# Second attention: ACT copies the bank turned one step earlier, then makes the exponential

## What is computed

```python
scores = (einsum('bhsc,btc->bhst', q_abs, kv) + einsum('bhsd,bxtd->bhst', q_pe, k_pe)) * SCALE
scores = where(causal, scores, finfo.min)
attn = softmax(scores, axis=-1)
x = einsum('bhst,btc->bhsc', attn, kv)
```

## Time and profile before

| | us |
|---|---|
| median of 3 runs | 1374.88 (1374.29 to 1378.86) |
| the profiled execution | 1376.57 |
| its span in the profile | 1374.8 |
| TensorE busy, share of the span | 1207.0, 88% |
| DVE busy | 887.0, 65% |
| ACT busy | 729.8, 53% |
| POOL busy | 535.7, 39% |
| mean granted TensorE clock | 0.932 |

### The profile page before, as it was taken

The page is one execution under the profiler, slowest core; times in us unless marked ns, Lnnn a source line. Parts: engine busy times, 40 slices in busy tenths (PEclk is TensorE's granted clock), DMA queues, the critical chain, the costliest instruction groups (busy, mean ns, idle before and its releaser), DMA issues. The chain is left out here.

```text
span 1374.8 us, 22122 instructions
## 1 busy us (share of the span) xinstructions
PE 1207.0 (88%) x7424; PEld 858.3 (62%) x7424; DVE 887.0 (65%) x2307; ACT 729.8 (53%) x1681; POOL 535.7 (39%) x561
## 2 busy tenths in 40 slices
PE   4798739999999889878599999999999999999878
PEld 3586714444444477667467777677767777676667
DVE  7767548899998345535477666667677666667501
ACT  2376303687777425453366656666666656665400
POOL 1244233435441100523065555455565555455200
PEclk9798855899999997999799999999999999999989
DMA  6670175446440285010211111101011111100091
GB/s 186 124 140 15 54 103 67 52 60 101 58 57 25 68 225 150 12 40 16 84 28 42 43 43 43 43 16 55 20 39 43 43 43 43 43 17 16 32 327 40
DMA packets 111057, 91.43 MB, mean 67 GB/s; under 512 B 49568, under 2 KB 101088, under 8 KB 109152
## 3 DMA queue, kind: packets, MB, share of 16 engines
q1 hardware_dynamic: 110944, 90.01, 28.6%
HBM read 50.92 MB, written 30.67 MB: 59 GB/s over the span
## 5 line engine op out<-in xcount | busy, mean ns | idle before, releaser
L988 POOL TENSOR_SCALAR a_p<-a_p,a_rl 128x128 f32<-128x128 f32 (+7 forms) x256 | 216.8, 849 | 332.0 <-DVE a_rl L930 331.7
L971 ACT ACTIVATE a_p<-psum,a_nm 128x128 f32<-128x128 f32 (+7 forms) x256 | 189.7, 741 | 58.4 <-DVE a_nm L924 56.7
L1485 ACT ACTIVATE a_pt<-psum 128x512 f32<-128x512 f32 (+3 forms) x384 | 168.1, 493 | 76.5 <-PE psum L1345 73.5
L1027 PE MATMUL psum<-ident,a_p 128*128 128x128 f32 x1152 | 175.7, 280 | 13.9 <-DVE a_pt L957 13.9
L957 DVE COPY a_pt<-psum 128x512 f32<-128x512 f32 (+1 forms) x192 | 114.6, 597 | 101.2 <-PE psum L1027 100.6
L955 ACT ACTIVATE a_pt<-psum 128x256 f32<-128x256 f32 (+2 forms) x192 | 87.6, 456 | 156.6 <-PE psum L1027 156.6
L1027 PEld LDWEIGHTS psum<-ident,a_p 128*128 128x128 f32 x1152 | 127.2, 140 | 62.6 <-issue 48.1
L1054 PE MATMUL psum<-a_pt,v 128*64 128x256 f32 (+1 forms) x1280 | 159.4, 370 | 2.3 <-ACT a_ot L1068 2.3
L1335 PE MATMUL psum<-a_op_k,a_op_q 64*128 64x512 f32 (+3 forms) x384 | 137.1, 456 | 23.8 <-DVE a_op_k L1451 22.7
L1345 PE MATMUL psum<-a_op_q,a_op_k 64*128 64x512 f32 (+3 forms) x384 | 129.9, 421 | 8.0 <-ACT a_pt L1485 6.1
L1345 PEld LDWEIGHTS psum<-a_op_q,a_op_k 64*128 64x128 f32 x384 | 64.1, 197 | 103.5 <-ACT a_pt L1485 86.8
(11 more groups left out here) (338 smaller groups left out, 2772.3 us busy)
## 6 DMA issues: line engine op xcount, KB each, us to landing
a_swap<-w_p SPq DMA_DIRECT2D x64, 128.0 KB, 2.3
ot_d<-a_ot SPq DMA_DIRECT2D x16, 512.0 KB, 4.5
o_ot<-ot_d SPq DMA_DIRECT2D x8, 1024.0 KB, 9.6
a_raw_q<-qk_d SPq DMA_DIRECT2D x48, 128.0 KB, 4.7
room<-qk_d SPq DMA_DIRECT2D x48, 128.0 KB, 7.8
w<-wf_d SPq DMA_DIRECT2D x16, 384.0 KB, 3.3
qk_d<-d_stage_h SPq DMA_DIRECT2D x64, 64.0 KB, 2.1
qk_d<-d_stage_l SPq DMA_DIRECT2D x64, 64.0 KB, 2.1
```

The source lines that it names most:

```text
L971: e.activation(s.p[:, t % NPB, 0:(i + 1) * P], C.score[t % 2][:, 0:(i + 1) * P], ACT.Exp, scale=-1.0, bias=s.nm[:, k:k + 1], accum_out=s.l ...
L988: e.tensor_scalar(s.p[:, t % NPB, 0:(i + 1) * P], s.p[:, t % NPB, 0:(i + 1) * P], s.rl[:, k:k + 1], 1.0, ALU.mult, ALU.mult).then_inc(s.no ...
L1027: ins = e.transpose(C.turn[par][:, (k - k0) * P:(k - k0 + 1) * P], s.p[:, tt % NPB, k * P:(k + 1) * P], C.ident[:, :])
L1485: e.activation(pt[:, k // G0 % NPT, hd, off:HALF], bank_b("score", g, k)[:, off:HALF], ACT.Exp, scale=-1.0).then_inc(exped, 1)
```

## The change

ACT's copy of a turned bank in slot t is that of the unit turned in slot t-1, not in slot t. DVE has had this order in all slots but the last of a group. The exponential of step t stays where it is, behind the copy of its slot; the output copy stays ahead of both. At the end of the stage the slots that run on after the last step (10 of them) take the copies that are left. Nothing is added or removed: as many copies, of the same shapes, with the same semaphores and counts, each a slot later in ACT's program.

```diff
 def softmax_act(e, C, s, n, t, later):
     core = s.core
     S = n * core.SI + t
-    evacuate(e, C, s, n, t, later, 1)
+    evacuate(e, C, s, n, t - 1, later, 1)
     if t < core.SI:
         c, hd, i = core.steps[t % core.SG]
         k = t % NST
```

## The result

The changed kernel takes 1405.51 us in the median of its runs (1399.15 to 1408.6), against 1375.38 for the kernel before in the runs beside it: a ratio of 1.0207, 95% interval 1.0176 to 1.0237. It is slower by 2.1%, 30.1 us between the medians. Its profiled execution took 1406.48 us, with a span of 1404.7, 29.9 more than the 1374.8 of before.

A forecast was written before the change was run, and what follows sets the result against it. TensorE was taken to bound the stage. 16 groups x 0.96 us (slot 12), 15 boundaries x 0.96 (slot 0) and 0.33 for the tail gave 30.1: median 1405.0 us, own range 1400 to 1409, wider range 1389 to 1416.

The forecast's parts named there:

- The mechanism: Slots 12 and 0: TensorE's odd-bank transposes wait for ACT's later copy (line 955), delaying the scores; 31 waits in all.
- both places: Slot 12, before score(13), and slot 0, before score(1): each 0.96 us late; slot 12 alone costing had chance 0.04, slot 0 alone 0.13.
- turn(15): TensorE's turn in slot 15: expected still to wait about 0.84 us for DVE, not absorbing slot 12's delay.
- The gain: Exponentials no longer waiting for their own slot's turn: value 0, bounds 0 and 13 us; rival "faster" had chance 0.05.
- The price of a place: Slots 12 and 0: delay of the next score by the later copy, its lag and the odd transposes, 0.96 us each.
- the lag from the end of ACT's copy to the transpose: Slots 12 and 0: taken as 0.15 us, from the tail's value products that waited for an ACT copy.
- The two checks beside it: Times from the ends of exp(11) and exp(15) to the scores waiting for them: 0.14 and 0.15 us.
- The edges: First group, last stretch and tail: late places at 0.96 us each, and 0.33 us for the tail.
- the tail: After the last group: value products 0.59 us later, last products 0.26 us earlier, +0.33 us in all.
- 1.00 throughout: TensorE's granted clock, expected to be still 1.00 in the changed kernel's trace.
- The sum: Whole stage: 15.4 us for slot 12, 14.4 for slot 0 and 0.33 for the tail, 30.1 us; chance 0.70.
- The walk past the other places: Other odd banks: turn(14) closest, 0.08 us late but hidden, copy(12) with more in hand; value 0, third-place rival 8 us, 0.08.

The follow-up runs named there:

- e3: Changed kernel's order, but the odd banks of slots 11 and 15 copied in their own slots again; 1375.46 us, ratio 1.0007 against the kernel before.
- e4: Kernel before, with only the odd banks of slots 11 and 15 copied a slot late; 1399.73 us, ratio 1.0199.
- e7: Kernel before, with ACT copying the even banks of slots 14 and 15, and odd banks of slots 5, 7, 9 a slot late; 1351.79 us.
- e1: Changed kernel's order, but slot 11's odd bank copied in its own slot again; 1385.24 us, ratio 1.0087 against the kernel before.
- e8: Kernel before, with ACT copying the even banks of slots 14 and 15, and slot 12's odd bank a slot late; 1356.67 us.
- e5: Changed kernel, with the output copy behind the bank copy in every slot; 1392.35 us, ratio 1.0144 against the kernel before.

## Why the prediction was right, and where its numbers were not

**The mechanism** held at both places. TensorE waits for line 955 in slots 12 and 0, at no other place of a regular group; exp(11) and exp(15) start when DVE is done, no earlier against their scores than before; turn(15) still waits 0.84 for DVE, so the delay of slot 12 passes through DVE's chain whole. e3 and e4 show both halves by themselves.

**The gain** was taken as 0 and is 0.07 us in each regular group, 1 us in all, and 0.75 in the last group. Between score(8) and score(9) 1.39 us lie in the trace of before (850.89 and 852.28) and 1.34 in the changed one (779.26 and 780.60); e7 gets 0.06 back from slots 5, 7 and 9 alone. I had called exp(11) and exp(15) the only exponentials that count, since I took every row of waiting to be theirs. exp(7) ended at the moment at which TensorE wanted it and held it up by less than a row shows.

In the last group it was a misreading of the earlier trace rows. Of the 15 waits of the matmul row for an exponential, one of 0.40 us is ahead of score(5) of the last group, for exp(3), which stands behind the copy of its own slot's bank. With that copy late (e3) the wait is gone, and score(5) starts 0.65 us earlier after turn(15) of the 15th group: 10.93 instead of 11.58. Rows of the kernel before, then of e3:

```profile
1264.77 0.60 ACT L955 ACTIVATE a_pt<-psum 128x512 f32<-128x512 f32 x1 [1.34 <-PE psum L1027]
1265.26 0.47 ACT L971 ACTIVATE a_p<-psum,a_nm 128x256 f32<-128x256 f32 x1
...
1265.88 0.50 PE L1006 MATMUL psum<-k10h,a_q10h 128*128 128x512 f32 x1 [0.40 <-ACT a_p L971]
```

```profile
1260.83 0.60 ACT L955 ACTIVATE a_pt<-psum 128x512 f32<-128x512 f32 x1 [0.46 <-PE psum L1030]
...
1261.29 0.48 PE L1009 MATMUL psum<-k10h,a_q10h 128*128 128x512 f32 x1
```

**The price of a place** was forecast as 0.96 and is 0.83. The term that was mis-sized is the lag from the end of ACT's copy to the transpose: 0.15 in the sum, 0.05 in the trace (copy(11) ends at 789.05 and the transpose starts at 789.10; copy(15) at 801.48, and 801.53). My row was from another instruction, the first product with the values. The two checks beside it, 0.14 and 0.15 after exp(11) and exp(15), were made from the end of the exponential; the read of its accumulator comes behind it and was left out, and from its end they would have been 0.05 or so. With 0.05 the sum gives 0.86; where the last 0.03 went is open.

**The edges** were forecast as one more place for the first group (0.96), two for the last stretch (1.92) and 0.33 for the tail, 3.2 in all, and took 1.28, 2.42 and 1.92, 5.6 in all. Of the 1.28 of the first group 0.45 arise ahead of the score at 5.1 us into the stage, before any bank is turned, and 0.83 are slot 12's. The 0.45 go with the clock: over the same nine matmuls it was 0.98 in the kernel before (first row) and 0.74 in the changed one.

```profile
686.83:688.36 1.53, 1.53 (x9) 1.28 (x9) 0.93 (x6) 0.97 (x5) 0.38 (x1) 0.98 0.00 0
688.66:690.64 1.98, 1.98 (x9) 1.72 (x9) 1.03 (x6) 1.11 (x5) 0.63 (x2) 0.74 0.00 0
```

The last stretch, from turn(15) of the 15th group to the last turn(0), holds three terms, of which I had one. It took 36.43 us before. In e4, with two late places and the exponentials as before, it took 38.09: 1.66 more, two places of 0.83. In e3, with neither place and earlier exponentials, it took 35.68: 0.75 less. In e1, with one place and earlier exponentials, it took 36.51, which is 36.43 + 0.83 - 0.75. In these three the clock stayed at 1.00. In the changed kernel the two places and the gain make 37.34, and it took 38.85. The 1.51 left are the clock's by this difference, and 0.75 of them were hidden by the gain.

The clock fell there and in the tail. In the last group there is no preparation between score(0) and turn(0); the wait for copy(15) is then 1.79 us, and in the 5 us from the row that ends it the granted clock is 0.66 of full, at the last boundary and in the tail, where I had said 1.00 throughout. In e1 and e4 the same wait of 1.79 left the clock at 1.00 at that boundary; in the tail of e4 it was 0.50, the lower of its two levels. First two stretches of the changed kernel, then two of e4:

```profile
1283.58:1288.58 5.00, 5.00 (x29) 3.50 (x31) 1.59 (x6) 1.83 (x6) 1.29 (x2) 0.66 0.02 3
1320.93:1325.93 5.00, 5.00 (x27) 2.95 (x27) 0.90 (x2) 1.09 (x2) 0.92 (x1) 0.66 0.00 0
```

```profile
1281.86:1286.86 5.00, 5.00 (x41) 3.74 (x42) 2.21 (x9) 1.89 (x6) 1.77 (x3) 1.00 0.01 3
1318.45:1323.45 5.00, 5.00 (x21) 3.14 (x23) 0.89 (x2) 0.75 (x2) 0.91 (x1) 0.50 0.00 0
```

**The sum** of 30.1 us agrees with the 29.9 of the spans by luck: its terms agree less well. The regular groups took 22.3 where 14 x 1.92 = 26.9 was forecast, the edges 2.4 more than forecast, and 2.0 came from outside the stage (1.83 and 0.20). The stage itself grew by 27.9 (623.6 to 651.5).

**The walk past the other places** said that copy(12) had more in hand than copy(13). Taken alone it is the other way about: e3 and e8 show 0.33 at turn(13) and no hole at turn(14). In the changed kernel neither shows, since score(13) comes late enough.

**ScalarE's budget.** The rule of the Trainium skill, ScalarE: Activation LUTs, section Rules for kernel authors, was used wrongly. The page gives its 0.3 us and 0.83 ns an element for an ACTIVATE whose bias is a pointer operand. The bank copies have no such operand, so their 0.60 and 0.39 neither bear the rule out nor speak against it, and the 34 us doesn't follow from it. The exponentials have one. By the rule, as an estimate, they take 0.94 us for 768 columns and 1.15 for 1024; the changed kernel's rows have 0.90 and 1.11, so there the trace agrees to 0.04.

## What to carry to other kernels

Before an instruction is moved behind another on an engine that looks as if it only waits, ask who waits for it: with one bank, a copy that is late for its reader is late for the next writer, and everything in that engine's program stands behind the write. An engine's idle time is worth something when it is given work from the chain that bounds (the copies of two slots moved from DVE to ACT, 1.2%), not when its own waiting is made to look shorter. The edges of a stage need a walk of their own: the last group, without a preparation, had a wait that no regular group has, and there the earlier exponential did pay. And where one wait covers another, as DVE's at turn(15) did for slot 13, the covered one comes back when the first is removed.

## What the runs showed of the hardware

The granted clock can be lower after waits of TensorE of 1.3 to 1.8 us, and need not be. Each of them comes a few microseconds behind shorter ones (at the last boundary of the changed kernel 0.84 and 0.37 us ahead of the 1.79), so no run shows what one wait alone does. Over the 5 us after the wait of 1.28 us in the tail the clock was 1.00 in the kernel before (1292.97 to 1297.97) and 0.67 in e3. After 1.52 us in e5 it was 0.66 at the last boundary and 1.00 in the tail. After 1.79 us it was 1.00 or 0.66 at the last boundary and 0.66 or 0.50 in the tail, in different kernels and executions. With the waits of 0.8 to 1.2 us in the regular groups it stayed up: the changed kernel has a mean of 1.00 over the 562 us of its 14 groups. What decides it is open; no run was made for it.

The first score of the stage varied between 675.8 and 685.1 us from execution to execution, with identical code ahead of it, while the length of a group repeated to 0.04 us within a trace (38.60 and 38.56 in turn, each to 0.02, in the kernel before, 40.16 to 40.19 in the changed one). For a change inside one repeated stage that length is the finer measure.
